# Pair products of the first chunk in two-sample matmuls, two loads moved, and a last layer in halves

## The reference

```python
bottom_mlp_output = bottom_output[:, 0, :]
interaction = jnp.einsum('bnd,bmd->bnm', bottom_output, bottom_output)
interaction_flat = interaction[:, _TRIL_R, _TRIL_C]
x = jnp.concatenate([bottom_mlp_output, interaction_flat, zero_pad], axis=1)
x = jax.nn.relu(x @ W0.T + b0)
...
return x @ W4.T + b4
```

## Time and profile before

| | us |
|---|---|
| median of 3 runs | 448.12 (446.96 to 448.62) |
| the profiled execution | 448.29 |
| its span, first to last instruction | 446.5 |
| TensorE matmul busy | 437.7 (98%) |
| VectorE busy | 253.7 (57%) |
| ScalarE busy | 172.0 (39%) |

### The profile page before, as it was taken

The page is one execution under the profiler, slowest core; times in us unless marked ns, Lnnn a source line. Parts: engine busy times, 40 slices in busy tenths (PEclk is TensorE's granted clock), DMA queues, the critical chain, the costliest instruction groups (busy, mean ns, idle before and its releaser), DMA issues.

```text
span 446.5 us, 13313 instructions
## 1 busy us (share of the span) xinstructions
PE 437.7 (98%) x5863; PEld 383.4 (86%) x5863; DVE 253.7 (57%) x499; ACT 172.0 (39%) x303; POOL 0.7 (0%) x6
## 2 busy tenths in 40 slices
PE   8999999999999999998999999999999999999996
PEld 7999987888788789997998778999998879999983
DVE  4877686849396468534256357736345567432335
ACT  3865443434254453331315345303215453330341
POOL 0000000000000000000000000000000000000000
PEclk9999999999999999999999999999999999999999
DMA  8985689798989657837982425987673003976300
GB/s 295 390 342 176 261 295 365 238 383 289 399 309 355 222 164 226 280 127 251 403 316 80 146 82 167 306 291 236 200 244 124 0 1 102 324 222 232 113 0 0
DMA packets 36778, 99.96 MB, mean 224 GB/s; under 512 B 3826, under 2 KB 5874, under 8 KB 35698
## 3 DMA queue, kind: packets, MB, share of 16 engines
q1 hardware_dynamic: 36722, 99.12, 64.0%
HBM read 82.33 MB, written 16.79 MB: 222 GB/s over the span
## 4 chain that ended last, share of the span: by engine, by line
PE 89%; DMA 4%; SPq 3%; DVE 2%; ACT 1%; issue 1%
PE work L1061 16%; PE work L1062 15%; PE work L1063 15%; PE acc L1061 8%; PE acc L1062 8%; PE acc L1063 8%; PE gps L1070 6%; PE gps L1061 3%; PE gps L1063 3%; PE gps L1062 3%; DMA xmid<-x_t 3%; SPq L390 2%; DMA ring<-w_parts 1%; PE acc L1088 1%; PE gps L1111 1%
## 5 line engine op out<-in xcount | busy, mean ns | idle before, releaser
L1061 PE MATMUL work<-featH,w0l 126*128 126x512 f32 (+5 forms) x160 | 57.6, 360 | 0.0
L1062 PE MATMUL work<-featH,w0h 126*128 126x512 f32 (+5 forms) x160 | 55.9, 349 | 0.0
L625 ACT ACTIVATE h2h<-act_out,bias 128x512 fp32r<-128x512 f32 x24 | 17.2, 718 | 99.4 <-DVE act_out L907 93.9
L1063 PE MATMUL work<-featL,w0h 126*128 126x512 f32 (+5 forms) x160 | 55.5, 347 | 0.0
L1061 PE MATMUL acc<-h2h,w2l 128*128 128x512 f32 x128 | 50.9, 397 | 0.0
L1062 PE MATMUL acc<-h2h,w2h 128*128 128x512 f32 x128 | 50.0, 391 | 0.0
L1063 PE MATMUL acc<-h2l,w2h 128*128 128x512 f32 x128 | 49.9, 390 | 0.0
L1061 PE MATMUL work<-th,ring 128*128 128x256 f32 x144 | 41.0, 285 | 0.0
L567 ACT ACTIVATE act_out<-work,bias 128x512 f32<-128x512 f32 (+1 forms) x40 | 25.7, 643 | 39.3 <-PE work L1063 39.3
L1062 PE MATMUL work<-th,ring 128*128 128x256 f32 x144 | 40.7, 283 | 0.0
L1063 PE MATMUL work<-tl,ring 128*128 128x256 f32 x144 | 40.7, 283 | 0.0
(11 more groups left out here) (125 smaller groups left out, 915.2 us busy)
## 6 DMA issues: line engine op xcount, KB each, us to landing
ring<-s_parts SPq DMA_DIRECT2D x48, 512.0 KB, 5.8
xraw<-x_t SPq DMA_DIRECT2D x50, 432.0 KB, 5.2
ring<-w_parts SPq DMA_DIRECT2D x36, 512.0 KB, 5.9
w_parts<-w1s SPq DMA_DIRECT2D x8, 1024.0 KB, 7.2
stage<-w_t SPq DMA_DIRECT2D x8, 512.0 KB, 6.8
s_parts<-sh SPq DMA_DIRECT2D x4, 1024.0 KB, 8.6
s_parts<-sl SPq DMA_DIRECT2D x4, 1024.0 KB, 11.3
xfirst<-x_t SPq DMA_DIRECT2D x9, 432.0 KB, 6.9
```

Of the source, the lines that this page charges most:

```text
L625: act.activation(h2h[:, pos % 2, :], full, ACT.Relu, bias=bias[:, row:row + 1]).then_inc(direct_hi, 1)
L1061: pe.matmul(dst, wl, ah, start=start, stop=False)
L1062: pe.matmul(dst, wh, ah, start=False, stop=False)
L1063: return pe.matmul(dst, wh, al, start=False, stop=stop)
```

## The change

- Slices 1, 2, 3, 5, 6, 7, 9, 10, 11 of the first chunk (`FIRST_HALVED`) take a third form: from `xpad`, two samples are the 64 weight columns and 54 moving columns of one matmul on one of two column tiles of 64. A slice is 16 matmuls. Their result is copied out by four ACTIVATEs, as in the padded form. Slices 3, 7 and 11, which were tiled, now need `pad_input` and the four copies. Slices 4, 8, 12, 14 stay padded, and 0, 13, 15 tiled.
- The quarters of W0 are loaded after slices 8, 11, 13, 14.
- `load_x0(c + 2)` stands behind the ring load of (2, 4) and not of (1, 2).
- In the last chunk, the second row tile of layer 3, its ReLU and split, layer 4 and the answer are done in two halves of 256 columns.

```diff
-FIRST_PADDED = [1, 2, 4, 5, 6, 8, 9, 10, 12, 14]
+FIRST_PADDED = [1, 2, 3, 4, 5, 6, 7, 8, 9, 10, 11, 12, 14]
+FIRST_HALVED = [1, 2, 3, 5, 6, 7, 9, 10, 11]
...
-        W0_AFTER = [8, 9, 11, 12]
+        W0_AFTER = [8, 11, 13, 14]
...
-                sp.wait_ge(y_done, c + 1)
+                sp.wait_ge(y_done, c + 1 + (c == LAST))
...
                         if (i, j) == (1, 2):
                             answer(c - 1)
-                            if later:
-                                load_x0(c + 2)
+                        if (i, j) == (2, 4) and later:
+                            load_x0(c + 2)
...
+                if p in FIRST_HALVED:
+                    for q in range(GROUP):
+                        rows = slice(q * QUAD, (q + 1) * QUAD)
+                        src = BANKS[FIRST_BANKS[p][0]][rows, 0:2 * FIRST_COLS].rearrange("p (g c) -> p g c", c=2 * INPUTS)
+                        last = act.activation(dst[rows], src[:, :, q % 2 * INPUTS:(q % 2 + 1) * INPUTS], ACT.Copy)
+                    last.then_inc(grams_out, 1)
+                    return
...
+            def relu_last():
+                n, row = nth(LAST, 3, 1, False), MT0 + MT1 + MT2 + 1
+                for part_no, part in enumerate((LEFT, RIGHT)):
+                    act.wait_ge(tile_done, tiles(LAST, 3, 1, False) + part_no)
+                    act.activation(act_out[:, slot(3, 1, False), part], acc[:, 1 + part_no, part], ACT.Relu,
+                                   bias=bias[:, row:row + 1]).then_inc(relu_done, 1)
...
+            def split_last():
+                n = nth(LAST, 3, 1, False)
+                for part_no, part in enumerate((LEFT, RIGHT)):
+                    full, hi, lo = act_out[:, slot(3, 1, False), part], h2h[:, 1, part], h2l[:, 1, part]
+                    dve.wait_ge(relu_done, n + 1 + part_no)
+                    dve.tensor_copy(hi, full).then_inc(hi_done, 1)
+                    dve.wait_ge(hi_done, rounded(LAST, 3, 1, False) + part_no)
+                    dve.tensor_tensor(lo, full, hi.bitcast(f32), ALU.subtract).then_inc(split_done, 1)
+                dst = y[:, :].rearrange("o (p s) -> o s p", s=SUBS)
+                for part_no, part in enumerate((LEFT, RIGHT)):
+                    dve.wait_ge(logits_done, LAST + 1 + part_no)
+                    ge(dve, out_done, 16 * LAST)
+                    two = slice(part_no * SUBS // 2, (part_no + 1) * SUBS // 2)
+                    dve.tensor_scalar(dst[:, two, :], (acc[0:1, 3, part] if part_no == 0 else work[0:1, 0, part]).rearrange("o (s p) -> o s p", p=SUB),
+                                      bias4[0:1, 0:1], None, ALU.add).then_inc(y_done, 1)
...
-            for p in (4, 5, 6):
+            for p in range(3, 8):
                 pad_input(p)
             pair_picks(0, 0)
...
             pad_input(10)
+            pad_input(11)
             pairs_lo_part(0, 0, True)
...
+                if p in FIRST_HALVED:
+                    for k in range(SLICE_GROUPS):
+                        for h in range(2):
+                            at = k * GROUP + 2 * h
+                            two = xpad[:, FIRST_PADDED.index(p) % PAD_SLOTS, at:at + 2, :]
+                            last = pe.matmul(banks[0][h * 2 * QUAD:(h + 1) * 2 * QUAD, k * 2 * INPUTS:(k + 1) * 2 * INPUTS],
+                                             two.rearrange("p b n -> p (b n)"), two[:, :, 0:INPUTS], start=True, stop=True,
+                                             tile_position=(0, h * 2 * QUAD))
+                    last.then_inc(gram_done, 1)
+                    return
...
+            def layer3_last():
...
+                for k in range(KT3):
+                    pe.wait_ge(split_done, nth(LAST, 2, k) + 1)
+                    last = rows_of(k, acc[:, 0, :], 0, slice(0, CHUNK))
+                    for n, part in enumerate((LEFT, RIGHT) if k < KT3 // 2 else ()):
+                        if k == 0:
+                            pe.wait_ge(relu_done, nth(LAST, 2, 1 + n) + 1)
+                        rows_of(k, acc[:, 1 + n, part], 1, part)
+                last.then_inc(tile_done, 1)
+                for n, part in enumerate((LEFT, RIGHT)):
+                    for k in range(KT3 // 2, KT3):
+                        last = rows_of(k, acc[:, 1 + n, part], 1, part)
+                    last.then_inc(tile_done, 1)
+
+            def layer4_last():
...
+                whole = acc[0:1, 3, LEFT], work[0:1, 0, RIGHT]
+                for k in range(MT3):
+                    for n, part in enumerate((LEFT, RIGHT)):
+                        at = n if k else 0
+                        pe.wait_ge(hi_done, rounded(LAST, 3, k, False) + at)
+                        pe.matmul(whole[n], w4s[:, k, 1:2], h2h[:, k, part], start=k == 0, stop=False)
+                        pe.matmul(whole[n], w4s[:, k, 0:1], h2h[:, k, part], start=False, stop=False)
+                        pe.wait_ge(split_done, nth(LAST, 3, k, False) + 1 + at)
+                        last = pe.matmul(whole[n], w4s[:, k, 0:1], h2l[:, k, part], start=False, stop=k == MT3 - 1)
...
```

## The result

The changed kernel took 446.5 us (median of 20 runs, 445.96 to 447.51), the kernel before 447.74 us in the runs beside it. The ratio is 0.9974, with a 95% interval of 0.9965 to 0.9982: 1.2 us faster, within the 0.5% that I called no change, and the time that was forecast. A few executions of these kernels, the one before as well, took 550 us and more; every median and ratio here is without them. The profiled execution took 447.07 us with a span of 444.9. The total hides that one part cost time, and that a rival came true for a moment.

What follows compares the result with a forecast made beforehand. The prediction took TensorE, 89% of the span, as the bound, with its waits at the start, a ring load and the end. Gains of 0.1 + 1.3 + 0.2 = 1.6 us gave 446.5 us; 8-in-10 range 444.8 to 449.0.

Steps and rivals of the forecast that it cites:

- The total: Whole kernel: 1.6 us off the median before, giving 446.5 us, 0.36% less; chance 0.60 of a change within 0.5%.
- Price of a slice: First chunk on TensorE: a two-sample slice costs 1.07 us, on a line between tiled 0.67 and padded 1.87.
- the dear form: Rival, slices 3 to 11: the two column tiles don't overlap; at 1.87 us a slice the total is 449.7; chance 0.10.
- Stage 1: First chunk up to the first dense tile: it starts at about 26.95, not 27.09, so 0.1 us gained.
- the two lists: First chunk: ScalarE's copies and VectorE's pads and picks, followed in order, let dense work start at about 26.95.
- The first rival: Start of dense work: loads decide, so it follows slice 12's landing, 1.36 us earlier; total 445.3; chance 0.20.
- the rule beside the earlier trace: First chunk: PSUM evacuation limits, so the stage wins nothing, against 1.3 us by TensorE's own saving alone.
- The clock: Rival: TensorE's waits drop it to 1.2 GHz for slices 9 to 11 and two dense tiles; 4.9 us lost; chance 0.04.
- x0: Chunk 1, P2 of set 2: moving this load removes TensorE's ring-load stall, 1.3 us once, bounds 0.6 to 1.5.
- The end: Last chunk's layers 3 and 4 by halves: last y at 443.8, not 444.0; 0.2 us gained, bounds 0 and 0.4.
- W0: Before slice 12: later quarters land it 1.36 us earlier, gaining 0.57 us and no more unless the pairs' chain moves.

Runs made afterwards that it cites:

- the second profile: Profile of the changed kernel run again unaltered, beside the same kernel with the old slices: 446.64 us, ratio 0.9978 to the kernel before.
- the kernel with six slices: The changed kernel with slices 3, 7 and 11 tiled again, leaving six in two-sample matmuls: ratio 1.0152 to the kernel before, 7 us slower.

## Why the prediction was right, point by point

**The total** was met: 446.5 forecast, 446.5 measured. That it was met to the tenth is luck. The forecast was 1.6 us below the median before as then shown (448.12), and measured in the same runs the gain is 1.2 from 447.74. Two terms were too large and one too small.

**Price of a slice (1.07 us taken):** right, 1.07. A line between the tiled and the padded form held for tiles of 64, so the dear form is refuted.

**Stage 1 (0.1 us gained taken; first dense tile at 26.95):** the two lists were right, the size and the premise not. At full clock the tile starts at 27.46. ScalarE's list runs nearly as forecast: first W0 quarter at 18.93 (18.60 in the second profile), forecast 18.5, and the copies of slice 11 until 26.5 (half clock) or 26.1, forecast 25.8. Slice 10's pad was done at 22.0 where I had 21.7. In the first profile that comes from ScalarE, whose copies ran 0.4 us late from slice 4 on (13.23 where I had 12.8); in the second from slice 7, whose pad started at 13.79 and not near 13.4. And I let the dense tile start with the end of the low parts, where 0.25 us pass between them (27.21 and 27.46 in the second profile). What I left out altogether is 0.3 us outside the span.

The premise that slice 12's landing decides when dense work begins came from one profile, in which its pad and slice 10's copies ended within 0.1 us of each other. By the table above it is the start of slice 10 that decides, and behind that ScalarE's copies. The first rival, by which slice 12's landing sets the dense tile 1.36 us earlier, did not come: that load was not what held it.

On the rule beside the earlier trace rows: the Trainium skill, "TensorEngine Tiling (Array Packing)", section "PSUM Bottleneck", says that tiling speeds up TensorE but not the evacuation of PSUM. The trace agrees, with ScalarE at 4.82 and 4.46 us of 5 and a dense tile that came no sooner. No run makes the copies alone cheaper, so how much of the stage they hold is not shown.

**The clock** was a rival at 0.04, for the whole stage and 4.9 us (a sum that counts two slices where it names three). It came in one profile, for part of 20 to 30 us, and costs 0.4 us there from slice 10 to the first dense tile (5.75 against 5.38). By the mean clock of 0.996 it may be 1 run in 10. In a run's time its cost is not resolved: the three runs have 447.1 to 447.5 us, and others at full clock have 447.2 to 447.4. The price of slice 11 rose in it from 1.04 to 1.86 us. The Trainium skill, "TensorE: Matmul & The Clock Gate", section "HAM oscillation", has the clock fall where TensorE idles between bursts. Here 1.8 us of wait stood ahead of the fall, and slice 8 ran at the lower level right behind the 2.9 us stop of the kernel with six slices. But waits of 1.34 us (two-sample slices alone) and 1.18 us (second profile) in the same place left the clock full, so what decides is not shown. The prediction's "no longer wait in mid-work" than 0.8 us at full clock was a misreading: the stall of 1.3 us of the earlier trace rows lies there too, and the clock stayed at 1.00 through it.

**x0 (1.3 us taken):** the step that was mis-sized. The mechanism is as told: with the move P2's load goes out 11 us sooner and the stall is gone in each profile. But the 1.3 us of the earlier trace rows was a large sample. Three kernels that kept x0's place had 0.7, 0.7 and no recorded wait in their profiles; the load took 4.7 us in the first two and 4.1 in the last, against 5.33 in the earlier trace rows. The starts are the better measure: from the transposes to the next product it is 1.81 us before, 1.21, 1.15 and 0.62 in the three, and 0.25 without the stall. The four losses are 1.56, 0.96, 0.90 and 0.37, 0.95 on average, and the timed gain is 0.9. My bounds held it.

**The end (0.2 us taken):** mis-sized the other way: 0.49 us in the profile, 0.5 timed, just above my bound. The two halves of y last 0.65 and 0.63 us but start 0.49 apart, so together they cost 1.12 and not 1.24. The first starts 1.73 us behind the last product, where I had 1.89. The 24 halved products cost the 0.15 us of my estimate.

**W0 (up to 0.57 alone):** 0.45 us timed, not clear of zero, and 0.2 to 0.6 in the profiles, by which of the three with the old start it is held against. Within the bound, but the bound came from the pairs, and what held was slice 10. With the new slices on top the gain is lost.

## What to carry to other kernels

Before making an instruction cheaper, write down the lists of the engines that feed and empty it: nine slices at 1.07 us in place of 1.87 or 0.67 bought nothing, while one slice, the one whose banks a later one waits for, moved the first dense tile by 0.9 us in the profile. One profile gives a stall once; where the stall is the difference of a landing and a need, hold several profiles of kernels with the same stage beside each other, and look for a distance that stays the same. And a change to a stream of tiny matmuls should be looked at for stops in the middle of a run: count the instructions up to each stop, and look for a transfer of instructions just ahead of its end. They moved the time by 7 us where the data flow was expected to be better.

## What was unexpected of the hardware

TensorE stopped for up to 4.9 us in runs of 27-column matmuls with their data present, always at a multiple of 256 instructions from the same point, and went on 1.2 to 1.5 us after a 16 KB transfer of instructions. Kernels with nine two-sample slices show 2.05 to 2.12 us between span and time, all others 1.77 to 1.84. Each of their four profiles has a transfer of instructions (queue 14, 8 KB) 1.7 us after the end of the span, three of them a second at 2.0 to 2.1, and none of the other profiles has one there. That this is the cause of the 0.3 us is likely but was not tested.
